# The transfers of an edge list, dealt out anew over the blocks of a graph network kernel

## What is computed

```
x = layernorm(x + five attention convolutions (4 heads of 32), softmax over the edges into a node)
x = layernorm(x + relational attention (4 edge types), softmax by type and destination)
x = layernorm(x + two degree-normalised sums: segment_sum(h[src] * norm, dst) + b, an elu between)
x = layernorm(x + leaky(segment_sum(edge_val * h[edge_col], edge_row) + bias))
```

## Time and profile before

| | us |
|---|---|
| median of 3 runs | 5794.07 (5793.05 to 5795.5) |
| the profiled execution's own time | 5796.47 |
| its span, first to last instruction | 5794.7 |
| GpSimd busy | 4078.2 (70%) |
| TensorE busy, matmuls | 3630.9 (63%) |
| VectorE busy | 3388.3 (58%) |
| ScalarE busy | 1522.0 (26%) |
| all list transfers on GpSimd, busy | 432.8 in 416 |

### The profile page before, as it was taken

How to read it: one execution, slowest core, us unless ns; L and a number is a source line. 1 busy time by engine, 2 the same in 40 slices (tenths; PEclk the granted TensorE clock), 3 DMA queues, 4 the chain that set the end, 5 groups by cost and what they waited for, 6 DMA issues and landing times. The chain is left out here.

```text
span 5794.7 us, 84655 instructions
## 1 busy us (share of the span) xinstructions
PE 3630.9 (63%) x17936; PEld 2901.8 (50%) x17937; DVE 3388.3 (58%) x9194; ACT 1522.0 (26%) x3590; POOL 4078.2 (70%) x4168
## 2 busy tenths in 40 slices
PE   5667756666677667666888746666644444446555
PEld 3556545553666356554566536656533333334334
DVE  7777756664666556655666466666443344336665
ACT  4334323432334224332454422222100010000000
POOL 4477577776777677777777667666577767766775
PEclk6877768877767777777898855555655555558778
DMA  7556265645556266535665433331122122211111
GB/s 238 172 173 182 87 205 171 189 126 150 176 173 179 78 197 184 171 104 176 175 180 164 106 73 69 66 70 42 40 53 53 53 62 52 53 48 57 52 53 52
DMA packets 631578, 681.11 MB, mean 118 GB/s; under 512 B 178675, under 2 KB 512969, under 8 KB 631145
## 3 DMA queue, kind: packets, MB, share of 16 engines
q0 software_dynamic: 166480, 384.64, 23.8%
q1 hardware_dynamic: 464792, 293.21, 17.4%
HBM read 620.51 MB, written 56.89 MB: 117 GB/s over the span
## 5 line engine op out<-in xcount | busy, mean ns | idle before, releaser
L618 POOL DMA_INDIRECT kvconv<-kv_tab,src_all x1664 | 1627.9, 978 | 645.0 <-issue 499.6
L618 POOL DMA_INDIRECT rowsg_<-h_tab,src_all x832 | 788.8, 948 | 322.5 <-issue 252.9
L632 POOL DMA_INDIRECT lst_tab<-pay,ord_now x416 | 432.8, 1040 | 215.1 <-issue 124.9
L618 POOL DMA_INDIRECT rows_r<-rel_tab,idx_r x416 | 419.4, 1008 | 202.8 <-issue 113.4
L618 POOL DMA_INDIRECT rowss_<-h_tab,dst_i_g x416 | 397.9, 957 | 161.0 <-issue 119.5
L618 POOL DMA_INDIRECT kvlast<-kv_tab,src_all x416 | 409.7, 985 | 133.4 <-issue 123.1
L1061 ACT ACTIVATE Sconv<-s8conv 128x512 f32<-128x512 fp8e4 x384 | 240.8, 627 | 396.1 <-PE pA1conv L1019 285.0
L1123 DVE TENSOR_TENSOR msgconv<-kvconv,sm_attEconv 128x512 f32<-128x512 f32 x416 | 286.1, 688 | 80.2 <-PE pA0conv L1019 27.7
L1019 PEld LDWEIGHTS pA0conv<-Sconv,msgconv 128*128 128x128 f32 x1664 | 300.7, 254 | 13.1
L1019 PEld LDWEIGHTS pA1conv<-Sconv,msgconv 128*128 128x128 f32 x1664 | 291.4, 247 | 17.0
L1019 PE MATMUL pA0conv<-Sconv,msgconv 128*128 128x128 f32 x1664 | 299.7, 340 | 0.0
(11 more groups left out here) (655 smaller groups left out, 8960.0 us busy)
## 6 DMA issues: line engine op xcount, KB each, us to landing
qwinconv<-q_tab SPq DMA_DIRECT2D x1664, 64.0 KB
kvconv<-kv_tab,src_all POOLq DMA_INDIRECT x1664
st8conv<-st_tab SPq DMA_DIRECT2D x52, 512.0 KB
s8conv<-s_tab SPq DMA_DIRECT2D x52, 512.0 KB
qwinlast<-q_tab SPq DMA_DIRECT2D x416, 64.0 KB
kv_tab<-stageconv_n SPq DMA_DIRECT2D x28, 512.0 KB
rowsg_<-h_tab,src_all POOLq DMA_INDIRECT x832
q_tab<-stageconv_n SPq DMA_DIRECT2D x28, 256.0 KB
```

The costliest lines, as they stand in the source:

```text
L618: nc.gpsimd.indirect_dma_start(rows[:, par * TG + t, :], None, tab, bass.IndirectOffsetOnAxis(ap=idx[:, g * TG + t:g * TG + t + 1], axis=0 ...
L632: nc.gpsimd.indirect_dma_start(lst_tab, bass.IndirectOffsetOnAxis(ap=ord_now[:, i:i + 1], axis=0), pay[:, i, :], None).then_inc(sem("liste ...
```

## The change

The same 416 list transfers are dealt out anew. Layers 1 to 3 list 26 (MID) instead of 30 in the edge block and 34 in the joint as before, so PER is 60. Layer 4 keeps 30 in its edge block, and the last joint lists 28 instead of 42. A relational group lists 6 instead of 5, but the last group none. The relational drain lists 50 instead of 53 and no longer waits for all of them. The remaining 22 are listed by GpSimd in the first degree joint, from the columns that are loaded already, and the wait for all 416 stands there. The sums: 34 + 3 * 60, 58, 72 and 72.

```diff
 JOINT = 34
+MID = 26
+PER = MID + JOINT
 DRAIN = 30
-PER = DRAIN + JOINT
+EACH = 6
+BEHIND_REL = 50
+LISTED = [JOINT + (CONVS - 2) * PER, DRAIN + 28, EACH * (GROUPS - 1), BEHIND_REL + 22]
+MOST = 72
 TW = 26
-EACH = 5
-LISTED = [JOINT + 3 * PER, DRAIN + 42, 0, EACH * GROUPS, 53]
-MOST = 72
...
-                    list_rows(pool, JOINT, 0 if isinstance(l, int) else DRAIN)
+                    list_rows(pool, JOINT, 0 if isinstance(l, int) else MID)
...
-                        list_rows(pool, DRAIN)
+                        list_rows(pool, MID if deg is None else DRAIN)
...
-                        order_in(sp, l * PER - DRAIN, PER)
+                        order_in(sp, l * PER - MID, PER)
...
-                        list_rows(pool, EACH, EACH * g)
+                        if g < LAST:
+                            list_rows(pool, EACH, EACH * g)
                     gather_all(pool, group)
-                    pool.wait_ge(sem("listed"), 16 * sum(LISTED[:4]))
-                    order_in(pool, sum(LISTED[:4]), LISTED[4], "ord_pool")
+                    pool.wait_ge(sem("listed"), 16 * sum(LISTED[:3]))
+                    order_in(pool, sum(LISTED[:3]), LISTED[3], "ord_pool")
                     pool.wait_ge(sem("ord_pool"), 32)
-                    list_rows(pool, LISTED[4])
-                    pool.wait_ge(sem("listed"), 16 * T)
+                    list_rows(pool, BEHIND_REL)
...
-                    order_in(sp, sum(LISTED[:3]), LISTED[3])
+                    order_in(sp, sum(LISTED[:2]), LISTED[2])
...
-        def norm_joint(tag, acc, rs, sb, pb, loads, w, put, scale_n=None, pre=None, shift=None, aside=None):
+        def norm_joint(tag, acc, rs, sb, pb, loads, w, put, scale_n=None, pre=None, shift=None, aside=None, lists=False):
...
             with nc.Block() as block:
+                if lists:
+                    @block.gpsimd
+                    def _(pool):
+                        list_rows(pool, LISTED[3] - BEHIND_REL, BEHIND_REL)
+                        pool.wait_ge(sem("listed"), 16 * T)
...
-                    norm_joint("n1_", acc, rs, sb, pb, [(wn[:, :], w2[0])], wn, put_rows, scale_n=dinv_n)
+                    norm_joint("n1_", acc, rs, sb, pb, [(wn[:, :], w2[0])], wn, put_rows, scale_n=dinv_n, lists=True)
```

## The result

The changed kernel takes **5775.37 us** (median of 9 runs, 5771.42 to 5781.38), the kernel before beside it on the same chip 5795.5 us (9 runs, 5791.64 to 5798.15): a ratio of **0.9966, 95% interval 0.9956 to 0.9976**, or 20 us less. The forecast was 5772.0, its range 5765 to 5781. The profiled execution took 5775.63 us with a span of 5773.8, against 5796.47 and 5794.7 before.

A forecast was written before the change was run, and what follows sets the result against it. The prediction took lists to cost time only in blocks that GpSimd ends last. Its terms, -17.2 - 11.8 + 6.9 = -22.1 us, gave 5774.4 for the profiled execution and 5772.0 for the median, range 5765 to 5781.

The forecast's parts named there:

- Which engine is last: At every block's end: a list costs time only where GpSimd is the last engine past its DRAIN.
- Term 1: Edge blocks of layers 1 to 3: four lists fewer each and a shorter tail, GpSimd still last; -17.2 us.
- Rival B: Middle edge blocks: the tail falls to that of gathers alone, 6.6 instead of 8.7 us; 5765.7 us in all, 6%.
- C: Rival on the edge blocks: their end doesn't follow the lists, the DRAIN waits for something else; 5789.2 us, 6%.
- Term 2: Last joint: 28 instead of 42 lists, saving until SyncE becomes the last engine; -11.8 us.
- Term 3: Relational groups: one more list behind the gathers of groups 0 to 11 goes into GpSimd's idleness; 0 us.
- Rival F: Relational groups: they become bound by GpSimd, its transfers exceeding the idleness; slower, 5812.8 us, 3%.
- Term 4: Relational drain: 50 instead of 53 lists and no wait for all, but ScalarE ends the block; 0 us.
- The feared point: Relational drain: GpSimd would become last only if its DRAIN grew by 13 us, as it starts 10 us earlier.
- Term 5: First degree joint: 22 lists, a wait for all and a DRAIN with work make GpSimd last; +6.9 us.
- Rival D: First degree joint: lists come every 1.42 us and the DRAIN lasts 9.3, costing +16.9; 5782.0 us, 5%.
- Rival E: First degree joint: seven VectorE adds each hold a list for their own 0.69 us, +4.8; 5776.8 us, 7%.

The follow-up runs named there:

- e1_mid26: Kernel before with 26 instead of 30 lists in the middle edge blocks, the twelve moved to relational groups and drain; 5776.33 us, ratio 0.9974.
- e2_last28: Kernel before with 28 instead of 42 lists in the last joint, the fourteen moved to the first degree joint; 5778.24 us, ratio 0.9978.
- e10_twelve: Changed kernel with six more list transfers in each of twelve relational groups, to a table nothing reads; 5789.51 us, ratio 0.9994 to the kernel before.
- e3_n22: Kernel before with 22 lists moved from the relational drain to the first degree joint; 5797.77 us, ratio 1.0011.
- e11_full: Changed kernel with lists dealt out further: 23 in middle edge blocks, seven a relational group, 11 in first degree joint; 5749.07 us, 0.9922 of kernel before.
- e8_after: The changed kernel itself run once more, nothing changed, beside the kernel before; 5771.24 us, ratio 0.9961.

## Why the prediction was right

**Which engine is last** was the main reading, and it held at each block that the forecast names: GpSimd at the middle edge blocks, SyncE in the last joint, ScalarE in the relational block, GpSimd in the degree joint. The joints behind the middle edge blocks were put at 0 and took 52.9 to 53.0 us, as before, but not by the way forecast: behind layers 2 and 3 VectorE was through after 49.0 and 49.1 us instead of 48.2, GpSimd after 51.8 and 51.0 instead of 52.9, and SyncE was last. That the two came out even was luck.

**Term 1, edge blocks, -17.2.** The tail of 8.7 us, taken between bounds of 6.6 and 9.0, came out as 8.7 in all three layers and in e1_mid26. Rival B (6.6) is out, and so is C: the end followed the lists. The term itself: -16.3 between the two profiles, of which layer 2 gave only 3.5: its last gather came 2.7 us later, as its gathers happened to run slower (the table shows 578 to 583 for the same code), and behind it 6.2 were saved. Three traces with 30 lists have a mean sum of 1752.5, five with 26 of 1737.4: **-15.0**, and e1_mid26's ratio gives -15.1. Both hold the gathers' scatter. The stretch behind the last gather, which the edit touches, went from 48.8 to 43.3 us: 5.55 a layer, **-16.7** in three. The forecast of 17.2 was right within 0.5 us there.

**Term 2, last joint, -11.8.** Measured 65.2 to 52.8 = -12.4 between the profiles, -12.7 by e2_last28's ratio. GpSimd's DRAIN was 2.333 us behind 28 lists, as 28 x 0.083 says. SyncE itself came 0.6 us earlier than before, inside the bound of 1 us, and 0.2 later in e2_last28. One step was mis-sized without effect: GpSimd's wait between the last list and its DRAIN was taken as 1.4 us and took 4.5, so that it was through 46.9 us behind the block's start instead of the forecast 45.2, still 5.9 before SyncE.

**Term 3, relational groups, 0.** 790.8 to 790.3 us. The waits shrank from 81.8 to 65.4 us for twelve lists' 15 us. Rival F (the groups become GpSimd's) has a mechanism that exists, as e10_twelve shows at +18 us. It begins between eight lists a group (+0.6) and twelve; with the 28.7 us of waits left at eight, two more in each group (28.7 / 12 / 1.27 = 1.9) would use them up, an estimate of ten, not six.

**Term 4, relational drain, 0.** ScalarE ends the block. One guess in it was loose: GpSimd's DRAIN did change its form, from 9.28 us behind the wait for all lists to 24.6 without it, but the time from the last list to its end, wait included, went from 10.6 us to 9.1. The feared point was 13 us of growth; GpSimd ends 16 us early.

**Term 5, first degree joint, +6.9.** Measured +6.3: GpSimd through 31.77 us behind the block's start, forecast 32.35. The DRAIN is 1.845 us (forecast 1.8). The pace was (4101.63 - 4074.89) / 21 = 1.273 us a list instead of the 1.30 taken; 21 x 0.03 = 0.6 is the whole difference. Rival D (1.42 a list and a DRAIN of 9.3) is out. Rival E too: all seven adds of 0.69 us lie beside lists, and each of the 22 lists took 0.96 or 0.97 us. The Trainium skill ("SBUF — State Buffer", section "SBUF: two separate sides") names VectorE operations in a 2-port performance mode or with two SBUF inputs. These adds have one input in PSUM, and no row says that they ran in such a mode; so the rows don't contradict the page, and the forecast was right to take no stretch. The prediction's other remark on it doesn't hold: it called the list of 3.49 us an agreement with the page, but that list ends at 1352.95, 1.39 us behind the RECIPROCAL's end at 1351.56, not some 115 ns. e3_n22 confirms the term at +6.4.

**The sum.** Between the profiles the touched stages give -16.3 - 12.4 - 0.5 + 6.3 = -22.9, against the forecast's -22.1; the untouched ones add 2.0 (the first edge block -3.6, layer 4's +1.6, the last degree joint +1.3, and smaller ones), so -20.9. Of the 3.4 us between 5775.4 and the forecast, 1.4 is the kernel before, whose median rose from 5794.07 to 5795.5 with more runs, and the rest is term 1 and such scatter.

## What to carry to other kernels

Where one engine has work that may be done anywhere, read for each block which engine passes its DRAIN last and by how much: work taken from a block pays only until the next engine is last, work put into one is free only until it makes its engine last. Waits of that engine inside a block were room as well on the chip of this result, until they were used up, and were not on the slower one; the busy shares show none of this. Look at the block behind, too: what keeps TensorE idle at a block's end can cost granted clock in the next. A deal balanced on one chip to a microsecond need not be balanced on another.

## What the runs showed of the hardware

**GpSimd's DRAIN costs 82 ns for each list issued since the last one, even when all of them are known to be done.** Behind a wait for all lists, in blocks without gathers, it took 0.94 us for 11, 1.192 for 14, 1.355 for 16, 1.845 for 22, 2.333 for 28, 2.660 for 32, 2.743 for 33, 2.825 for 34 and 3.477 for 42: a line of 82 ns a list from a start of some 0.04 us. In the edge blocks the tail behind 416 gathers and 23, 24, 26, 30 and 32 lists was 8.48, 8.55, 8.72, 9.04 and 9.20, the same slope. The relational drain does not follow it: 31 and 50 lists left tails of 8.5 and 9.1 us, and behind a wait for all, with the block's gathers, the DRAIN took 9.28 us for 53 lists before and for 58 in e11_full.

**What stretches a list.** In the last joint of the changed kernel, lists and VectorE's work beside them (start, duration):

```profile
3251.45 1.86 POOL L634 DMA_INDIRECT lst_tab<-pay,ord_now  x1 [0.30 <-issue]
...
3264.89 2.05 POOL L634 DMA_INDIRECT lst_tab<-pay,ord_now  x1 [0.30 <-issue]
```

```profile
3252.17 1.02 DVE L1411 CAST ends_f_j<-ends_i_j 128x1664 f32<-128x1664 int32 x1
...
3265.28 1.54 DVE L1429 TENSOR_SCALAR mask_r<-t_f_j 128x1248 bf16<-128x1248 f32 x1
```

The lists end at 3253.31 and 3266.94, both 0.12 us behind the VectorE operation beside them (3253.19 and 3266.82). So a CAST and a TENSOR_SCALAR can hold a list to their own end. The Trainium skill ("SBUF — State Buffer", section "SBUF: two separate sides") measured a release some 115 ns behind VectorE's end, and the 0.12 us agree. It isn't always so plain: a list from 3259.97, beside another such TENSOR_SCALAR until 3261.40, ended at 3262.04, 0.64 us behind it, and the one beside the RECIPROCAL ended 1.39 us behind it. What makes the difference isn't shown. The seven adds of the degree joint stretched no list. Which property of the operation decides was not measured by itself.

**TensorE's clock at the start of the degree joint.** SyncE came 27.1 us behind the block's start in the changed kernel, 25.5 before. Stretches of 4 us (then busy time of each engine, PEclk as the third number from the end), after and before:

```profile
4074.50:4078.50 4.00, 4.00 (x7) 1.63 (x8) 1.01 (x2) 0.63 (x1) 2.90 (x3) 0.50 0.07 17
4078.50:4082.50 4.00, 4.00 (x24) 3.52 (x23) 1.17 (x4) 2.18 (x3) 2.90 (x3) 0.75 0.03 2
```

```profile
4104.00:4108.00 4.00, 4.00 (x12) 1.84 (x12) 1.30 (x2) 0.63 (x1) 0.00 (x0) 0.63 0.06 16
4108.00:4112.00 4.00, 4.00 (x30) 3.34 (x29) 1.02 (x4) 2.81 (x5) 0.00 (x0) 1.00 0.00 0
```

The granted clock reached 2.4 GHz (1.00) after 8 us instead of 4. The edit is not the cause: the same kernel once more (e8_after) has SyncE at 25.3 us, and in its first 4 and next 4 us:

```profile
4072.76:4076.76 4.00, 3.73 (x9) 1.67 (x10) 0.94 (x2) 0.63 (x1) 2.50 (x3) 0.60 0.07 17
4076.76:4080.76 4.00, 4.00 (x33) 3.52 (x32) 1.38 (x4) 2.46 (x4) 3.09 (x4) 1.00 0.03 2
```

So the clock's rise varies between executions of the same code. It cost nothing here, because GpSimd was last; in e11_full, where SyncE is last, it is in the block's 27.4 us.
